# Softmax scores in three bf16 parts, four maxima units moved to the entry of the error attention, and routers on unnormalised rows, in a two-layer transformer kernel

## The chip, the core and the metric

The kernel runs on one core of one Trainium2 chip. A core has five engines that run their own instruction streams in order and meet only at semaphores: TensorE (PE, matrix products and transposes), VectorE (DVE), ScalarE (ACT), GpSimd (POOL) and SyncE (SP), which here issues nearly all DMAs. The metric is the device time of one execution in microseconds (us); the kernel before took a median of 610.33 us.

## The reference

Four sequences of 512 tokens with 128 features go through six steps, each on layer-normalised rows and added to the rows x:

```
x += 0.5 * ffn(norm(x))           # weights rounded to -1, 0, 1; exact gelu; 128 -> 512 -> 128
x += attention(norm(x))           # 16 heads of 8 features
x += 0.5 * ffn(norm(x))
x += 0.5 * experts(norm(x))       # 8 experts, relu, 128 -> 512 -> 128
x += linear_attention(norm(x))
x += 0.5 * experts(norm(x))
```

The attention is a sum of two. With q and k projected and v = the normalised rows, `y_ar = softmax(causal(q k^T / sqrt 8)) v`. The second works on the errors `e[t] = v[t+1] - y_ar[t]`: `y_ma = tril(qa ka^T) e`, where qa and ka are a leaky relu of q and a sigmoid of a third projection k2. Both go through one output projection.

In the experts step a router takes `softmax(row Wr)`, sends each of the 2048 tokens to its best expert, keeps the first 256 tokens of each expert in token order, and multiplies an expert's answer by the probability.

## The kernel before

**Stages.** Batch means one of the four sequences, tile 128 of its tokens. The entry (0 to 108 us of the profile) does the first feed-forward layer and the projections of all batches. The softmax attention follows batch by batch (to 162, 217, 272 and 312 us), then the second feed-forward layer with the first router (to 370), the experts (to 414), the linear attention with the second router at its end (to 566) and the second experts. The order of every engine is written out by hand in functions of the same name for each engine, such as `attention(b)` for PE (L1729), ACT (L902), DVE (L1238) and POOL (L691).

**Softmax scores.** A head has 8 features, so a full-precision product is made from halves: `split` (DVE, L1158) rounds q and k to float32r, `low_parts` (POOL, L638, through `low` at L601) takes the remainder. Each operand is written to DRAM three times by `stack` (SP, L363), as (high, low, high) for q and (high, high, low) for k, so that 24 contracted rows per head give high x high, low x high and high x low. A 25th row carries minus the maximum of the query's scores against a row of ones in DRAM, so that the exponent needs no other subtraction. Each head takes 32 of 128 partitions, and four heads make a set. One operand of a set stands as a block diagonal in `ring` (zeros cleared by POOL's `clear_ring`, L583), the other in `x_sets` or `m_sets`; the loads are `load_exp_set` (L368) and `load_max_set` (L376), five DMAs each. The zero and one rows in DRAM are stored at the start (L352 to L361).

**Maxima.** A query's maximum must be known before its scores are made. So PE makes all scores twice. In the first pass ten units of a set (pairs of a query tile and a key tile, 4 heads x 128 keys = 512 columns, `max_scores`, L1627) go through two PSUM banks, and DVE reduces each (`maxima`, L1169). The four units on the diagonal get a mask added by one more matmul, in bf16. For the first batch this is done in the entry, partly with four banks (`wide_scores`, `wide_maxima`); for batch b + 1 it is done beside the attention of batch b, placed by `MAX_BESIDE`. When all 40 units of a batch are reduced, `max_of_tiles` (DVE, L1186) makes the maximum over tiles, `max_turn` (PE, L1656) transposes it, `max_t` (ACT, L868) copies it out of PSUM, and `max_row` (SP, L414) writes the rows of maxima into `ring`.

**The loop.** For each set PE makes five units of two score matmuls (`scores`, L1662, two units ahead), ACT takes the exponent (L909), POOL clears the forbidden half of the diagonal (L669), and PE multiplies by the values (`answers`, L1674, groups of 8 small matmuls). Between these stand the maxima units of the next batch. `turn_answers` and `answers_divide` turn the answers of a set and divide them by their sums.

**Error attention.** After the last set, PE does `ma_scores(b, 0)`, turns the last answers, turns the maxima, turns y_ar (it waits for the copy of the maxima, since both use the bank `turn[1]`), and then goes through four tiles: state, `ma_scores` of the next tile, `ma_answers`. DVE masks the scores of each tile (L1267).

**Routers.** For each batch: moments (DVE, L1070), the reciprocal root on POOL (`rsqrt`, L587), `normalise` (L1075), transposes (PE), copy (ACT), `logits` (PE, L1571, fp32 matmuls of 8 columns), `choose` (DVE, L1105), `ranks` (PE, L1577), `place` (DVE, L1122), and `scatter` (POOL, L603, indirect DMAs that write the rows to their expert). In the first router PE does the transposes and logits of batch b - 1 inside `output` of batch b (`route`, L1782). In the second the last batch stands alone at the end of the linear attention (`turn_exit`, L2007). Where PE would be idle, `stay_awake(n)` (L1525) issues n bf16 matmuls of 512 columns whose result is not used.

## Time and profile before

| | |
|---|---|
| three runs | 607.28, 616.01, 610.33 us, median 610.33 |
| profiled execution | 613.04 us, its span 611.2 us |
| granted TensorE clock, mean over the span | 0.95 of full speed |
| busy: PE, DVE, ACT, POOL | 501.7, 340.9, 214.8, 243.7 us |
| chain that ended last | PE 55%, DVE 18%, POOL 7%, issue 6%, ACT 6%, DMA 5% |
| DMA | 79.86 MB, mean 131 GB/s |

Busy time and chain are of the one profiled execution; the span is from its first to its last instruction, and the execution's time has 1.8 us more. The chain is followed back from the last instruction, at each step to what released it. PEld is the loading of weights into PE, which can run beside a matmul. A matmul's end is modelled: those that follow each other overlap in the listing, so the distance between starts, not the duration, says what one costs.

### The profile page before, as it was taken

To read this page: it belongs to the slowest core of one execution; us is meant where nothing else is said; L and a number is where in the kernel's file an instruction comes from. 1 tells how busy PE (TensorE), PEld (TensorE's weight loads), DVE (VectorE), ACT (ScalarE), POOL (GpSimd) and SP (SyncE) were. 2 spreads that over 40 slices of the span, in tenths; PEclk is the share of its full clock that TensorE was granted. 3 is DMA by queue.
4 is the path that set the end of the run, shared out by engine and by line. 5 is a ranking of instruction groups with operands and counts; after the bars stand their busy time and mean duration, and the time that the engine had idled before them with its cause. 6 is when DMAs were issued, how large, how long until landed. Compare 5 with 4: busy or idle time off the path is not lost.

```text
span 611.2 us, 10402 instructions
## 1 busy us (share of the span) xinstructions
PE 501.7 (82%) x3827; PEld 321.1 (53%) x3827; DVE 340.9 (56%) x912; ACT 214.8 (35%) x298; POOL 243.7 (40%) x292
## 2 busy tenths in 40 slices
PE   0787776899999999989888978947887797898893
PEld 0564432444644654464467735943455575653692
DVE  4653586477487757752235651315697888842131
ACT  0446232554456455448644501202231311100120
POOL 5576365133342433336412465552221130332153
PEclk9996798899999999999999989998998999977997
DMA  8306989564156225405699322312857272111220
GB/s 258 154 22 198 314 249 294 153 187 123 34 133 186 63 62 157 121 17 154 156 155 261 112 96 86 105 38 76 237 160 192 68 223 80 54 52 36 87 64 10
DMA packets 73730, 79.86 MB, mean 131 GB/s; under 512 B 11010, under 2 KB 50563, under 8 KB 73424
## 3 DMA queue, kind: packets, MB, share of 16 engines
q1 hardware_dynamic: 70824, 73.15, 42.6%
q0 software_dynamic: 2560, 5.58, 2.6%
q8 instruction: 31, 0.51, 0.4%
q10 hardware_dynamic: 296, 0.47, 0.2%
q14 instruction: 19, 0.16, 0.1%
HBM read 44.07 MB, written 35.72 MB: 131 GB/s over the span
## 4 chain that ended last, share of the span: by engine, by line
PE 55%; DVE 18%; POOL 7%; issue 6%; ACT 6%; DMA 5%; SPq 2%; POOLq 0%; DVEq 0%; ACTq 0%
PE ps_pair L1514 18%; PE ps_accum L1514 16%; PE ps_max_pair L1514 15%; POOL sb_rstd L592 2%; DVE sb_work L1409 2%; DVE sb_stats L1070 2%; DVE sb_mpart L1173 2%; SPq L366 1%; PE ps_turn L1522 1%; POOL xe_scr L612 1%; PE ps_turn L1695 1%; PE ps_max_pair L1522 1%; DMA sb_cols<-in_bias_cols 1%; DMA sb_expert_rows<-xe_scr 1%; DVE sb_y_tmp L1079 1%
## 5 line engine op out<-in xcount | busy, mean ns | idle before, releaser
L1173 DVE TENSOR_REDUCE sb_mpart<-ps_max_pair 128x4 f32<-128x512 f32 x132 | 88.0, 688 | 41.2 <-PE ps_max_pair L1514 40.8
L909 ACT ACTIVATE sb_work<-ps_pair 128x1024 f32<-128x1024 f32 x80 | 81.1, 1025 | 61.5 <-PE ps_pair L1514 60.7
L1514 PE MATMUL ps_max_pair<-sb_ring,sb_m_sets 128*128 128x512 f32 x146 | 64.7, 471 | 8.9 <-DVE sb_mpart L1173 5.4
L669 POOL TENSOR_SCALAR_AFFINE_SELECT sb_work<-sb_work 128x512 f32<-128x512 f32 (+1 forms) x48 | 37.8, 790 | 65.7 <-ACT sb_work L909 65.7
L1514 PE MATMUL ps_pair<-sb_ring,sb_xsets 128*128 128x512 f32 x160 | 57.4, 445 | 3.5 <-ACT sb_work L909 1.4
L1514 PE MATMUL ps_pair<-sb_ident_bf,sb_ones_bf 128*128 128x512 bf16 x185 | 49.1, 421 | 12.3 <-DMA sb_x<-y_scr 8.0
L1514 PE MATMUL ps_accum<-sb_work,sb_v_aug 128*32 128x128 f32 (+3 forms) x768 | 57.9, 400 | 1.1 <-POOL sb_work L669 1.1
L1514 PEld LDWEIGHTS ps_max_pair<-sb_ring,sb_m_sets 128*128 128x128 f32 x146 | 27.0, 192 | 45.5 <-DVE sb_mpart L1173 28.1
L1409 DVE TENSOR_TENSOR sb_work<-ps_pair,sb_cst 128x1024 f32<-128x1024 f32 x32 | 37.5, 1213 | 2.5 <-PE ps_pair L1514 2.5
L1514 PEld LDWEIGHTS ps_pair<-sb_ident_bf,sb_ones_bf 128*128 128x128 bf16 x185 | 19.5, 108 | 35.5 <-issue 10.2
L612 POOL DMA_INDIRECT xe_scr<-sb_exit_rows,sb_slot_all x16 | 15.9, 996 | 54.5 <-DVE sb_slot_all L1154 50.8
L1514 PEld LDWEIGHTS ps_pair<-sb_ring,sb_xsets 128*128 128x128 f32 x160 | 28.1, 194 | 15.5 <-issue 6.6
L590 POOL TENSOR_SCALAR sb_ve<-sb_mv 128x4 f32<-128x4 f32 x24 | 5.5, 231 | 69.5 <-DVE sb_mv L1073 63.8
L1514 PE MATMUL ps_pair<-sb_y_tmp,sb_mw 128*128 128x256 f32 x128 | 30.7, 383 | 2.0 <-ACT sb_y_tmp L971 2.0
L1514 PEld LDWEIGHTS ps_accum<-sb_work,sb_v_aug 128*32 128x32 f32 x768 | 17.8, 113 | 23.9 <-issue 18.5
L1514 PE MATMUL ps_pair<-sb_xs,sb_w1r 128*128 128x512 f32 x64 | 22.2, 474 | 9.6 <-DVE sb_xs L1089 6.0
L1353 DVE TENSOR_SCALAR sb_work<-ps_pair 128x512 f32<-128x512 f32 x16 | 10.9, 681 | 27.6 <-PE ps_pair L1514 27.6
L1514 PEld LDWEIGHTS ps_pair<-sb_y_tmp,sb_mw 128*128 128x128 f32 x128 | 23.1, 190 | 5.5 <-ACT sb_y_tmp L971 3.0
L592 POOL TENSOR_TENSOR sb_rstd<-sb_ve,sb_cst 128x4 f32<-128x4 f32 x24 | 25.0, 1041 | 2.0
L1514 PE MATMUL ps_pair<-sb_ring,sb_ka_stk 128*128 128x512 f32 x64 | 22.1, 461 | 2.9 <-DVE sb_work L1409 2.4
L688 POOL TENSOR_SCALAR_AFFINE_SELECT sb_work<-sb_work 128x1024 f32<-128x1024 f32 x16 | 17.5, 1092 | 17.6 <-ACT sb_work L900 17.6
L1514 PE MATMUL ps_max_pair<-sb_add_q_bf,sb_ident_bf 128*128 128x512 bf16 x59 | 23.5, 398 | 0.0
(251 smaller groups left out, 981.2 us busy)
## 6 DMA issues: line engine op xcount, KB each, us to landing
sb_ka_stk<-mk_scr SPq DMA_DIRECT2D x16, 512.0 KB
sb_expert_rows<-xe_scr SPq DMA_DIRECT2D x16, 258.0 KB, 2.8
sb_m_sets<-q_scr SPq DMA_DIRECT2D x16, 256.0 KB
xe_scr<-sb_cst SPq DMA_DIRECT2D x4, 1024.0 KB, 13.0
sb_mw<-in_mw SPq DMA_DIRECT2D x16, 256.0 KB, 5.7
sb_xsets<-k_scr SPq DMA_DIRECT2D x15, 256.0 KB
q_scr<-sb_qs SPq DMA_DIRECT2D x12, 256.0 KB, 3.8
k_scr<-sb_ks SPq DMA_DIRECT2D x12, 256.0 KB, 4.0
```

The source lines that it names most:

```text
L366: sp.dma_start(scr[:, c], hi_lo[:, part, :].bitcast(F32)).then_inc(kept, 16)
L592: pool.tensor_tensor(rstd[i][:], ve[i][:], const("minus_half"), ALU.pow).then_inc(s["rstd"], 1)
L612: pool.indirect_dma_start(xe_scr[m], bass.IndirectOffsetOnAxis(ap=slot_all[:, i:i + 1], axis=0), rows_out[m][b][:, t, :], None).then_inc(s ...
L669: pool.affine_select(weights, weights, [[0, weights.shape[1]], [0, HL], [1, P]], ALU.is_ge, 0.0, base=0, channel_multiplier=-1).then_inc(s ...
L688: pool.affine_select(part, part, [[0, 2 * HL], [1, P]], ALU.is_ge, 0.0, base=-1, channel_multiplier=-1).then_inc(s["ma_zeroed"], 1)
L909: act.activation(unit_slots(i), pair[u % 2][:], ACT.Exp, scale=SCALE).then_inc(s["exp_done"], 1)
L1070: dve.bn_stats(stats[i][:, t, :], src[:, t, :]).then_inc(s["stats"], 1)
L1173: dve.tensor_reduce(mpart[:, m // NPAIR, m % NPAIR, :], max_banks[m % 2][:].rearrange("p (h k) -> p h k", h=HL), AX.X, ALU.max).then_inc(s ...
L1353: dve.tensor_scalar(work[:, n % 2, 1, :], pair[n % 2][:, 1, :], 0.0, None, ALU.max).then_inc(s["h_relu_v"], 1)
L1409: dve.tensor_tensor(work[:, n % 4].rearrange("p a (h q) -> p (a h) q", h=HL), pair[n % 2][:].rearrange("p a (h q) -> p (a h) q", h=HL), bc ...
L1514: return pe.matmul(dst, lhsT, rhs, start=start, stop=stop, skip_group_check=True)
L1522: last = pe.transpose(tile(dst, t), src[:, t, 0:D], ident)
```

## The change

1. **Scores.** q and k are kept as three bf16 parts (high, middle, least), whose sum is the float32 value. Six products (parts of 8 rows each, so 48 rows) replace three; a head takes 64 partitions, and two heads ("a half") stand in one matmul's block diagonal. The scratch in DRAM is bf16, each operand is stored by three DMAs of contiguous parts, and a set is loaded by four DMAs. The maxima become two bf16 rows (high and rest), which DVE makes by one copy and one subtraction more in `max_of_tiles`. POOL fills `x_sets` with ones, so the rows of ones and two of three rows of zeros in DRAM go. The middle part costs a subtraction and a cast per operand (`rest`), on DVE for batches 0 and 1, on POOL for 2 and 3.
2. **Units.** A maxima unit is one matmul of 2 heads x 256 keys (or two of 256 columns), a set has ten units with 18 matmuls, masks included, and 12 score matmuls. The columns per set stay at 12,288.
3. **Entry of the error attention.** Four units of the last set leave the loop: two stand before `ma_scores(b, 0)`, two after the turn of the last answers. Their reduces and `max_of_tiles` stand on DVE after the first mask and the first state, `max_turn` stands at tile 1 and has another bank, and y_ar is turned after `ma_scores` of tile 1.
4. **Routers.** Wr loses its column mean once (one matmul, one DVE operation), so that logits can be taken from rows that are not normalised: the choice of the expert needs no scale, and the logits are scaled before the exponent. Transposes and logits so follow the sum directly. In the first router the logits of batch b - 1 are made in the first step of the next output, the ranks in the third. In the second, the 27 idle matmuls before `turn_exit` become 4. The 32 idle matmuls ahead of each experts stage become 8 before the places, 24 after them and 14 after the scatter.

The core of the diff:

```diff
-MAX_PAIRS = [(qt, kt) for qt in range(NT) for kt in range(qt + 1)]
+MAX_UNITS = [(0, "3ab"), (0, "3cd"), (0, "2ab"), (0, "1ab"), (1, "3ab"), (1, "3cd"), (1, "2ab"), (1, "1ab"), (0, "2c0a"), (1, "2c0a")]
 MAX_BESIDE = [(1, 0, 0), (1, 1, 1), (1, 0, 0), (1, 0, 1), (1, 0, 2)]
+MAX_BESIDE_LAST = [(1, 0, 0), (1, 1, 1), (1, 0, 0), (1, 0, 0), (0, 0, 0)]
+MAX_LEFT = [NS * NPAIR - 4, NS * NPAIR - 2, NS * NPAIR]
...
-        q_scr = dram("q_scr", [B, H, 4, HD, T])
+        q_scr = dram("q_scr", [B, H, HD, PARTS, T], BF16)
...
+        def rest(eng, b, i):
+            full, parts, high, least = operands[i]
+            eng.wait_ge(s["split_hi"], 2 * b + i + 1)
+            if i == 0:
+                eng.wait_ge(s["ma_q"], b + 1)
+            eng.tensor_tensor(full[:], full[:], parts[:, high], ALU.subtract).then_inc(s["split_part"], 1)
+            eng.wait_ge(s["split_part"], 4 * b + 2 * i + 1)
+            eng.tensor_copy(parts[:, 1], full[:]).then_inc(s["split_part"], 1)
...
+            def stack_parts(parts, scr, kept, runs):
+                rows = scr.rearrange("h d c t -> (h d) c t")
+                for c, (first, last) in zip((0, 3, 5), runs):
+                    sp.dma_start(rows[:, c:c + last - first], parts[:, first:last]).then_inc(kept, 16)
...
             def load_exp_set(b, hs):
...
+                for j in range(HP):
+                    rows_of = slice(PR * j, PR * j + PARTS * HD)
+                    sp.dma_start(x_ring[rows_of, i, :, j], half_rows(q_scr, b, hs, j)).then_inc(done, 16)
+                    sp.dma_start(x_sets[rows_of, i], half_rows(k_scr, b, hs, j)).then_inc(done, 16)
...
             def low_parts(b):
+                if b >= 2:
+                    rest(pool, b, 0)
+                    rest(pool, b, 1)
+                for i, (full, parts, high, least) in enumerate(operands):
+                    pool.wait_ge(s["split_part"], 4 * b + 2 * i + 2)
+                    pool.tensor_tensor(parts[:, least], full[:], parts[:, 1], ALU.subtract).then_inc(s["split_lo"], 1)
...
-            clear_ring(0, 2)
+            clear(x_ring[:])
...
-            clear_ring(2, 3)
+            pool.memset(ring[:, 2].bitcast(F32), 0.0)
+            clear(m_ring[:, 0])
...
+            pool.wait_ge(s["ffn_h"], NF * B)
+            pool.memset(x_sets[:], 1.0).then_inc(s["x_ones"], 1)
             low_parts(B - 1)
...
             def max_of_tiles(b):
...
+                dve.tensor_copy(max_high[:], mneg[:, :, :, 0]).then_inc(s["max_parts"], 1)
+                dve.wait_ge(s["max_parts"], 2 * b + 1)
+                dve.tensor_tensor(mneg[:, :, :, 1], mneg[:, :, :, 0], max_high[:], ALU.subtract).then_inc(s["max_parts"], 1)
...
             def before_attention(b):   # DVE
                 if b:
                     split(b - 1, 0)
+                    query_features(b - 1)
                     split(b - 1, 1)
-                    query_features(b - 1)
+                    if b <= 2:
+                        rest(dve, b - 1, 0)
+                        rest(dve, b - 1, 1)
...
             def scaled_logits(r, norm):   # new, DVE
+                dve.wait_ge(s["rstd"], norm + 1)
+                dve.tensor_tensor(r8[1][:], r8[0][:], rstd[r % B % 2][:].unsqueeze(2).broadcast_to([P, NT, E]),
+                                  ALU.mult).then_inc(s["lg_scaled"], 1)
...
             def after_attention(b):   # DVE
                 ffn_x(B + b, x[b], old)
-                moments(norm_second(B + b), old, b % 2)
-                if b:
-                    choose(b - 1, accum[1])
-                normalise(norm_second(B + b), old, rows_out[0][b], b % 2)
+                n = norm_second(B + b)
+                moments(n, old, b % 2)
+                choose(b, accum[1])
+                normalise(n, old, rows_out[0][b], b % 2)
+                scaled_logits(b, n)
                 if b + 2 < B:
                     low(B + b + 2)
-                if b:
-                    place(b - 1, b - 1, accum[1], slot_all[:, NT * (b - 1):NT * b])
+                place(b, b, accum[1], slot_all[:, NT * b:NT * (b + 1)])
...
             def attention(b):   # PE, after the loop over the sets
+                if ahead:
+                    max_scores(b + 1, MAX_LEFT[0], MAX_LEFT[1])
                 ma_scores(b, 0)
                 turn_answers(b, NS - 1)
                 if ahead:
-                    max_turn(b + 1)
-                pe.wait_ge(s["y_norm"], NS * b + NS)
-                if ahead:
-                    pe.wait_ge(s["max_t_evac"], b + 2)
-                turn_tiles(turn[1], y_ar).then_inc(s["yar_mm"], 1)
+                    max_scores(b + 1, MAX_LEFT[1], MAX_LEFT[2])
...
                         ma_scores(b, t + 1)
+                    if t == 0:
+                        if ahead:
+                            pe.wait_ge(s["smax_red"], (NM + NT) * (b + 1) + MAX_LEFT[2] - 1)
+                        pe.wait_ge(s["y_norm"], NS * b + NS)
+                        turn_tiles(turn[1], y_ar).then_inc(s["yar_mm"], 1)
+                    elif t == 1 and ahead:
+                        max_turn(b + 1)
                     ma_answers(b, t)
...
             pe.wait_ge(s["experts_loaded"], 16 * 2 * E)
+            stay_awake(8, pair[1][:, 0])
             pe.wait_ge(s["rank_j"], B)
-            stay_awake(32, pair[1][:, 0])
+            stay_awake(24, pair[1][:, 0])
+            pe.wait_ge(s["scattered"], 16 * NT * B)
+            stay_awake(14, pair[1][:, 0])
             experts(0)
...
             project_out(B - 1)
-            stay_awake(27, pair[0][:, 0])
+            stay_awake(4, pair[0][:, 0])
             turn_exit(B - 1)
```

## Rows read from the trace of the kernel before

**Rows 1.** Page, part 1: busy us of each engine, share, instructions.

```profile
PE 501.7 (82%) x3827; PEld 321.1 (53%) x3827; DVE 340.9 (56%) x912; ACT 214.8 (35%) x298; POOL 243.7 (40%) x292
```

**Rows 2.** Windows: us, busy PE, PEld, DVE, ACT, POOL, clock, DMA share, GB/s.

```profile
75.00:95.00 20.00, 15.36 (x53) 6.95 (x51) 16.38 (x19) 7.84 (x13) 12.96 (x10) 0.99 0.82 248
163.00:203.00 40.00, 38.88 (x240) 18.41 (x238) 29.34 (x58) 22.14 (x23) 14.40 (x21) 1.00 0.49 139
...
540.00:567.00 27.00, 23.81 (x116) 11.97 (x115) 6.76 (x38) 1.99 (x4) 9.23 (x10) 0.81 0.15 50
```

**Rows 3.** Chain of waits, batch 1's sets: start us, us, what.

```profile
167.03 1.00 PE ps_accum L1514 x8
...
177.26 1.00 PE ps_accum L1514 x8
186.95 0.99 PE ps_accum L1514 x8
```

**Rows 4.** Timeline of PE inside one set: start us, us, instruction.

```profile
182.28 0.50 PE L1514 MATMUL ps_max_pair<-sb_ring,sb_m_sets 128*128 128x512 f32 x1
182.62 0.62 PE L1514 MATMUL ps_pair<-sb_ring,sb_xsets 128*128 128x512 f32 x2
183.08 0.39 PE L1514 MATMUL ps_max_pair<-sb_ring,sb_m_sets 128*128 128x512 f32 x1
```

**Rows 5.** Chain of waits through the second router.

```profile
546.34 5.83 PE ps_pair L1514 x27
552.17 0.45 PE ps_max_pair L1522 x4
...
553.28 1.07 PE ps_max_pair L1514 x8
...
555.52 0.52 PE ps_max_pair L1514 x14
...
565.91 2.73 DMA sb_expert_rows<-xe_scr
```

**Rows 6.** Page, part 5: count, then busy us, mean ns, idle before.

```profile
L1173 DVE TENSOR_REDUCE sb_mpart<-ps_max_pair 128x4 f32<-128x512 f32 x132 | 88.0, 688 | 41.2 <-PE ps_max_pair L1514 40.8
...
L1514 PEld LDWEIGHTS ps_max_pair<-sb_ring,sb_m_sets 128*128 128x128 f32 x146 | 27.0, 192 | 45.5 <-DVE sb_mpart L1173 28.1
...
L1514 PEld LDWEIGHTS ps_pair<-sb_ident_bf,sb_ones_bf 128*128 128x128 bf16 x185 | 19.5, 108 | 35.5 <-issue 10.2
```

**Rows 7.** Chain of waits through the first router's last batch.

```profile
350.56 0.70 DVE sb_wide_rows L1101
...
354.27 1.34 DVE sb_wide_rows L1079 x4
...
362.05 0.96 POOL xe_scr L612
```

**Rows 8.** Timeline of all engines where batch 0's error attention begins.

```profile
150.37 0.55 DVE L1191 TENSOR_REDUCE sb_mneg<-sb_mpart 128x16 f32<-128x16 f32 x4
...
152.34 0.63 PE L1522 MATMUL ps_max_pair<-sb_cst,sb_y_ar 128*128 128x128 f32 x4 [0.76 <-ACT sb_qs L876]
...
153.69 1.23 DVE L1267 TENSOR_TENSOR sb_work<-ps_pair,sb_cst 128x1024 f32<-128x1024 f32 x1 [0.17 <-PE ps_pair L1514]
...
155.29 1.17 PE L1514 MATMUL ps_pair<-sb_qa_pad,sb_ka_stk 128*128 128x512 f32 x4
```

**Rows 9.** Timeline of POOL in the entry: one of its fills.

```profile
24.14 1.81 POOL L585 MEMSET sb_ring<- 128x2048 f32 x1
```

**Rows 10.** Timeline of the entry: batch 2's remainder and its stores.

```profile
75.51 1.27 POOL L601 TENSOR_TENSOR sb_qs<-sb_qf,sb_qs 128x512 fp32r<-128x512 f32 x1 [5.94 <-DVE sb_qs L1162]
...
76.88 2.13 SPq L366 DMA_DIRECT2D q_scr<-sb_qs  x3
```

**Rows 11.** Chain of waits in the entry: a load of the last set.

```profile
91.75 3.90 DMA sb_m_sets<-q_scr
```

**Rows 12.** Timeline of PE: idle matmuls ahead of the second experts.

```profile
558.14 9.81 PE L1514 MATMUL ps_pair<-sb_ident_bf,sb_ones_bf 128*128 128x512 bf16 x32 [2.11 <-DVE sb_slot_all L1154]
```

More of the change, by code:

```diff
@@ L183, in build @@
         xs = [sb("xs_0", [P, 2, T], F32R)]
[L184 removed]
+        with nc.sbuf_tensor("sb_xsets", [P, 2, HP, T], BF16) as x_sets:
             pass
@@ L196, in build @@
         yT = w1
+        with nc.sbuf_tensor("sb_q_parts", [P, 3, T], BF16) as q_parts:
+            pass
+        with nc.sbuf_tensor("sb_max_rows", [P, T], BF16) as max_rows:
+            pass
         qs = sb("qs", [P, 2, T], F32R)
+        with nc.sbuf_tensor("sb_k_parts", [P, 3, T], BF16) as k_parts:
+            pass
         ks = sb("ks", [P, 2, T], F32R)
@@ L206, in build @@
             pass
+        with nc.sbuf_tensor("sb_x_ring", [P, 2, HP, HP, T], BF16) as x_ring, nc.sbuf_tensor("sb_m_ring", [P, 2, HP, HP, T], BF16) as m_ring:
+            pass
         ring = sb("ring", [P, NS, HL, T], F32R)
@@ L414, in max_row @@
             def max_row(b, hs):
-                sp.dma_start(ring[3 * HD:3 * HD + 1, hs % 2].bitcast(F32),
-                             mT[HL * hs:HL * hs + HL].bitcast(F32)).then_inc(s[f"xset{hs % 2}"], 16)
+                for j in range(HP):
+                    r = PR * j + PARTS * HD
+                    sp.dma_start(x_ring[r:r + 2, hs % 2, :, j], max_of_heads(hs, j)).then_inc(s[f"xset{hs % 2}"], 16)
             def keep_values(b):
@@ L743, in _ @@
             add_bias(norm_first(2 * B - 1), B - 1, 0, s["ffn_base"])
-            for b in range(2):
+            rsqrt(norm_second(B), 0)
+            for b in range(1, B):
+                scatter(0, b - 1, 0, 2)
                 rsqrt(norm_second(B + b), b % 2)
-            for b in range(2, B):
-                scatter(0, b - 2, 0, 2)
-                rsqrt(norm_second(B + b), b % 2)
-                scatter(0, b - 2, 2, NT)
-            for b in range(B - 2, B):
-                scatter(0, b)
+                scatter(0, b - 1, 2, NT)
+            scatter(0, B - 1)
             pool.wait_ge(s["rank_b"], 2 * B)
@@ L949, in _ @@
             act.wait_ge(s["max_t_evac"], 1)
-            act.dma_start(ring[3 * HD:3 * HD + 1, 0].bitcast(F32), mT[0:HL].bitcast(F32)).then_inc(s["xset0"], 16)
+            for j in range(HP):
+                r = PR * j + PARTS * HD
+                act.dma_start(x_ring[r:r + 2, 0, :, j], max_of_heads(0, j)).then_inc(s["xset0"], 16)
             act.wait_ge(s["mq_kept"], 48 * B)
@@ L1240, in attention @@
                 if b + 1 < B:
-                    at = [9] + [NPAIR * (hs + 1) + 3 for hs in range(NS - 1)] + [NM]
+                    at = [9] + [NPAIR * (hs + 1) + 3 for hs in range(NS - 1)] + [MAX_LEFT[1]]
                     maxima(b + 1, 0, 1)
@@ L1269, in attention @@
                                       bc(const("key_before"), 2 * HL), ALU.mult).then_inc(s["ma_masked"], 1)
+                    if t == 0 and b + 1 < B:
+                        maxima(b + 1, MAX_LEFT[1], MAX_LEFT[2])
                     if t < NT - 1:
@@ L1610, in before_attention @@
                 last = b == B - 1
+                if last:
+                    pe.wait_ge(s["wr_mid"], 1)
                 output(b, (lambda i: max_scores(0, i, i + 1)) if last else None)
@@ L1668, in scores @@
                     pe.wait_ge(s["exp_done"], NX * b + u - 1)
+                k_of, q_of = x_sets[:, hs % 2], x_ring[:, hs % 2]
                 for a in range(2):
-                    kt, qt = EXP_UNITS[i][a]
-                    last = mm(pair[u % 2][:, a, :], tile(x_sets[:, hs % 2], kt), ring[:, hs % 2, :, qt * P:(qt + 1) * P])
+                    if one_key_tile(i):
+                        kt, qt = EXP_UNITS[i][0]
+                        last = mm(pair[u % 2][:, a, :], tile(k_of[:, a], kt), q_of[:, a, :, qt * P:(qt + 2) * P])
+                    else:
+                        kt, qt = EXP_UNITS[i][a]
+                        for p in range(HP):
+                            last = mm(pair[u % 2][:, a, p * 2 * P:(p + 1) * 2 * P], tile(k_of[:, p], kt),
+                                      q_of[:, p, :, qt * P:(qt + 1) * P], start=p == 0)
                 last.then_inc(s["st_mm"], 1)
@@ L1743, in attention @@
                         scores(b, u + 2)
-                    m = NPAIR * hs + sum(map(sum, MAX_BESIDE[:i]))
-                    ends = [m + sum(MAX_BESIDE[i][:n]) for n in range(4)]
+                    beside = MAX_BESIDE if hs < NS - 1 else MAX_BESIDE_LAST
+                    m = NPAIR * hs + sum(map(sum, beside[:i]))
+                    ends = [m + sum(beside[i][:n]) for n in range(4)]
                     if ahead and (u or b == 0):
@@ L1791, in route @@
                         logits(b - 1, f - 1, accum[1], xnT[(b - 1) % 2])
+                    elif i == 2:
+                        ranks(b - 1, accum[1])
                 output(f, route if b else None)
```

292 lines of the change are left out of this document (160 added, 132 removed).

## The prediction, made before the changed kernel ran

> **What bounds the kernel now.** I read the summary of the page first: TensorE is busy for 82% of the span, VectorE for 56% [rows 1]. The table of stages says where that holds: in the attention (163 to 203 us) PE works 38.9 of 40 us, while in the entry (75 to 95) PE, VectorE and POOL work 15.4, 16.4 and 13.0 of 20, and in the router before the second experts (540 to 567) the clock is down to 0.81 of full speed [rows 2]; there engines take turns, and before the first experts too. The chain of waits then gives the pace. One set of four heads takes 9.7 us while the next batch's maxima are made beside it (177.26 to 186.95), and 10.2 us as the first of a batch (167.03 to 177.26) [rows 3]; the last batch's sets, which have no maxima beside them, are shorter. So the attention is priced on PE, and the other three places by their chains.
>
> **Scores in bf16 (A).** One set now issues 10 score matmuls and 10 maxima matmuls of 512 columns in float32r and 4 bf16 masks. The change issues 12 and 18 in bf16, some of 256 columns, but the columns are the same: 24 x 512. So only spacing can change. Two float32r matmuls that begin at 182.62 are followed by the next at 183.08, 0.23 us each; the first after a group of answers takes 0.34 (182.28 to 182.62) [rows 4]. 27 bf16 matmuls of 512 columns in a row take 5.83 us, 0.216 each, and 14 of 8 columns, each with its own weights, 0.52 us, 0.037 each; 8 of 8 columns in fp32 take 1.07, 0.13 each [rows 5]. So 20 x 0.02 = 0.4 us and five group heads x (0.11 - 0.04) = 0.35 us are to be had per set, less about 0.1 for six more matmuls: 0.65. VectorE gets none of this: ten reduces of 0.69 [rows 6] and a division keep it busy for 7.3 us of each 10 [rows 2], of what would be 9.04 us, and PE may be only two maxima ahead. I take 0.5. In the first set of batches 1 and 2 DVE also adds the last answers, takes moments and normalises (0.70 and 1.34 for the first and the last of these in [rows 7], the moments between them), which with 7.3 fills the 10.2, so no gain there. 10 x 0.5 + 4 x 0.4 in the last batch = **-6.6** (bounds: 0, if the reduces set the pace; -11, if all 16 sets get everything).
>
> The profile shows weight loads of 0.19 us in float32r and 0.11 in bf16, and that most of the former are hidden in the 0.23 [rows 4, 6]. The Trainium skill (TensorE: Matmul & The Clock Gate, sections Weight-path perf modes and Back-to-back issue gap) says that 128 weights not in fp32 load about twice as fast, and that load and matmul together set the spacing; the first agrees with the two rows, and by the second the whole difference would count, which is the first rival below.
>
> **Error attention (B).** Two of the four moved units leave the last set's loop (two matmuls with the waits around them, 0.5 each, so -1.0); they are issued where PE idles 0.76 us for the maxima's copy. But DVE now does, between its first mask and its second (153.69), two reduces (1.4), the reduction over tiles (0.55) and, new, a copy and a subtraction of 256 words (0.3 with their waits, an estimate) [rows 6, 8]. The second mask so ends some 1.5 us later than at 154.9, near 156.4, and PE, which needs it for the scores that begin at 155.29, waits 0.9 us; transposing the answers (0.45, as in [rows 5]) is no longer covered. The 32-row transpose has its own bank, and the rows of maxima land well before the next batch's scores. Net +0.3 for each of three batches, +0.45 in the last: **+1.3** (bounds: -2, if the stall is covered; +5, if none of the moved units is).
>
> **Entry (C).** In the first 43 us POOL's fills of 2048 float32 words take 1.81 us and stand right ahead of two rsqrt [rows 9]. The change adds a fill of 2048 bf16 words to each, and makes the fill of 4096 words before them (3.6 us by this row) one of bf16. If a fill goes by elements this is +3.6, if by bytes +1.8 - 1.8 = 0; no row has a bf16 fill of any size, so I take +2.0, between the two. The middle part costs two subtractions and two casts per batch. On DVE a pass over 512 float32 words takes 0.70 [rows 7], a cast perhaps 0.4, so 2.2 us for each of batches 0 and 1; DVE is busy for 16.4 of 20 us later in this stage [rows 2], and I let a quarter through, +1.0. For batches 2 and 3 they are on POOL, whose subtraction took 1.27 [rows 10]. For batch 2, SP waits for it to store q at 76.88; q's three stores would start 4.7 us later (two subtractions of 1.27, two casts of an estimated 1.1), and behind them stand the loads of set 2, the feature stores and the load of set 3 (the chain's DMA of 3.90 us at 91.75), which releases PE at 95.7 [rows 10, 11]. The three stores each keep their bytes, a set needs four loads (384 KB) instead of five (448 KB), so some 1.7 us of the 4.7 is won back: +3.0. The DMA engines are 82% busy here [rows 2], and 2 MB of zeros are not stored any more: -1.0 for shorter landings. The fill of ones, batch 3's four operations and the later fills are covered by that load and what follows it, since the scores start near 108 us. Together **+5.0** (bounds 0 and +18: both batches' POOL work in full, 4.7 and 4.7 with 1 for the fill of ones, the fills by elements, 3.6, and DVE's 4.4). The router's centred weights (one small matmul, one DVE operation, hidden by the fills' wait) and a second DMA for each row of maxima (on a queue with slack of a whole set) cost nothing.
>
> **Routers (D).** In the first, the last batch's rows wait after their sum (350.56, 0.70) for moments, POOL's rsqrt and a normalise of 1.34 at 354.27, and only then come transposes, copy, logits, choice, ranks and places; scatters start at 362.05 [rows 7]. Unnormalised, the transposes follow the sum at 351.26 directly, and the steps take what the second router shows: transposes 0.45, copy 0.6 (552.62 to 553.28), logits 1.07, choice 1.1 (554.35 to 555.52), ranks 0.52 and places 2.1 (556.04 to 558.14) [rows 5, 12]. 351.26 + 0.45 + 0.6 + 1.07 + 1.1 + 1.34 (normalise, ranks beside it) + 0.2 (scaling) + 2.1 and 0.3 of gaps is 358.4, and rsqrt runs beside it. But the earlier batches' choices now wait for logits inside the next output, ahead of DVE's places and sum; by the same rows the last sum is 1.0 us later. Gain 2.7. In the second, PE runs 27 idle matmuls (5.83) between projection (546.34) and transposes (552.17), and places are done at 558.14 [rows 5, 12]. After 546.34: 0.7 (sum) + 0.45 + 0.6 + 1.07 + 1.1 + 1.1 (normalise) + 0.2 + 2.1 + 0.3 of gaps = places at 553.9 instead of 558.1, so 4.2. Together **-6.9** (bounds: -9; +1, see the second rival). The 14 idle matmuls behind the scatter take 3.0 us at 0.216, about as long as the rows take to come (2.73 for the last DMA [rows 5], and its issue).
>
> **Sum.** -6.6 + 1.3 + 5.0 - 6.9 = -7.2 us. The profiled execution took 613.0 us (span 611.2 and 1.8 around it), which gives 605.8; it is 2.7 above the median of the three runs, 610.3, which gives **603 us**.
>
> **Rivals.** *Weight loads count in full.* 0.19 - 0.11 on 20 loads is 1.6 to 1.7 us per set, 12 sets and half as much in four: A = -24, time **586**. For it: five heads of groups per set expose 0.11. Against: within a run 0.23 holds load and matmul. The Trainium skill's rule on spacing, named above, is this one. 0.15.
>
> *VectorE paces, and the routers' gain is lost.* A falls to -1.5, since 7.3 us of reduces and division with two banks leave PE waiting; and the choice of batch b, which waits for logits inside the next output, makes DVE the bound of the feed-forward stage; or PE is granted the lower clock (the 32 idle matmuls at 558.14 took 9.81, 0.31 each, clock 0.81 in this stage [rows 2, 12]) and 14 more take 6 us, 3 too many: D = -2. Then **613**. So the scores would be cheaper on an engine that isn't the limit. 0.22.
>
> *POOL becomes the entry's bound.* Place: between the last split and SP's stores, 75 to 108 us. If nothing of it is covered C is 18 and the time **616**, slower. It decides from C = 12.2, that is, from an attention that starts later than about 120 us. Against: POOL is busy 13 of 20 us there [rows 2], and SP's own queue, not POOL, fills the chain from 77 to 91 us. 0.10.
>
> **Numbers.** Forecast 0.53, on its own 596 to 609. A measurement of this kernel can tell about 2%, 12 us, from no change. Faster by more (under 598): the first rival's 0.15 and a quarter of the forecast's, 0.28. Slower by more (over 622.5) takes the third rival together with A near 0: 0.04. Within: 0.68. The range 590 to 614 leaves out most of the first rival and the third.
>
> **What would show it.** A: sets of about 9.2 us, 0.22 between matmuls, PE's weight loads near 0.1; sets still at 9.7 with PE waiting for the reduce say the second rival, under 8.5 the first. B: PE waiting for DVE's second mask near 8 us after the last answers. C: first scores at about 113 us; at 108 or less my price of POOL was wrong, over 120 the third rival is right. D: scatters of the last batch 2 to 4 us sooner after the sum, places 8 us after the last projection. The forecast fails if attention and entry both come out on one side of their terms.

## The result, and the profile after

| | before | after |
|---|---|---|
| median of 20 runs, us | 610.38 (607.28 to 617.09) | 614.66 (610.81 to 618.41) |
| ratio, 95% interval | | 1.0053 (1.0031 to 1.0076) |
| profiled execution, us | 613.04, span 611.2 | 611.52, span 609.8 |

The change makes the kernel slower, by 0.3 to 0.8% (of the two medians, 4.3 us); 603 was forecast, in a range to 614. The profiled execution of after is among the fastest of its twenty and that of before among the slower ones, so the two traces are compared stretch by stretch and not by their sums.

Page after, part 1 (the columns of [rows 1]). PE is 17.6 us less busy; the time does not follow, so PE now waits somewhere.

```profile
PE 484.1 (79%) x3917; PEld 300.6 (49%) x3917; DVE 348.2 (57%) x937; ACT 214.9 (35%) x301; POOL 254.8 (42%) x303
```

Windows of after, for the stretches of [rows 2]: entry, attention, second router.

```profile
75.00:95.00 20.00, 17.13 (x58) 7.18 (x56) 12.64 (x15) 6.90 (x11) 13.31 (x13) 0.82 0.61 200
168.00:208.00 40.00, 36.41 (x264) 14.83 (x264) 29.11 (x58) 22.31 (x24) 15.02 (x22) 1.00 0.51 129
541.00:566.00 25.00, 21.70 (x133) 11.29 (x126) 7.88 (x47) 1.98 (x4) 9.23 (x10) 0.89 0.20 66
```

In the attention PE was busy for 38.9 of 40 us, now for 36.4. The chain of waits through one set of batch 1 shows what took PE's place; in [rows 3] the set from 177.26 to 186.95 held PE alone.

```profile
183.81 0.26 DVE sb_rcp L1298
...
184.09 0.30 DVE sb_y_ar L1300
...
184.47 0.46 POOL sb_e_pad L727
184.93 0.41 POOL sb_v_next L728
185.34 1.07 POOL sb_work L715
...
186.55 0.43 PE ps_accum L1593 x8
...
194.88 1.06 POOL sb_work L715
```

PE's answers wait for POOL's clear of the forbidden half (L715); that stands on POOL behind two subtractions (`errors`, L727 and L728), which wait for DVE's division of the set before. From clear to clear it is 9.54 us, the period of the later sets of a batch: only 0.15 less than the 9.69 of [rows 3]. The timeline of after shows the same clear with its shape and PE's wait (start, us, instruction, in brackets the idle time ahead and its releaser).

```profile
185.08 0.60 PE L1593 MATMUL ps_pair<-sb_x_ring,sb_xsets 128*128 128x512 bf16 x2
185.30 1.10 POOL L715 TENSOR_SCALAR_AFFINE_SELECT sb_work<-sb_work 128x1024 f32<-128x1024 f32 x1
185.52 0.38 PE L1593 MATMUL ps_max_pair<-sb_m_ring,sb_m_sets 128*128 128x512 bf16 x1
186.55 0.43 PE L1593 MATMUL ps_accum<-sb_work,sb_v_aug 128*32 128x128 f32 x8 [0.54 <-POOL sb_work L715]
```

It clears 1024 columns, two blocks of the diagonal at once. The starts at 185.08 and 185.52 answer to [rows 4]: two bf16 matmuls in 0.44 us, 0.22 each, as forecast. The weight loads fell to 0.1 us (page after, part 5, against 192 and 108 ns in [rows 6]).

```profile
L1593 PEld LDWEIGHTS ps_max_pair<-sb_m_ring,sb_m_sets 128*128 128x128 bf16 x176 | 15.7, 99 | 50.4 <-DVE sb_mpart L1236 21.5
```

In the entry, the first exponent starts at 116.05 us instead of 108.67. The chain of waits of after shows where: a fill of 2048 bf16 words, the stores of batch 2, the last load (they answer to [rows 9 to 11]: 1.81 us, 76.88, 91.75), and behind the load the last step of the maxima (L1259) and two DMAs that ACT issues for the rows of maxima (L999).

```profile
25.67 1.80 POOL sb_m_ring L627
...
80.48 1.16 POOL sb_qf L362
...
81.70 0.68 POOL sb_q_parts L364
82.38 1.13 POOL sb_kf L362
...
83.56 0.61 POOL sb_k_parts L364
84.17 1.13 POOL sb_q_parts L687
...
85.38 0.33 SPq L407
...
97.46 3.69 DMA sb_m_sets<-q_scr
...
109.19 0.44 DVE sb_mneg L1259 x4
...
111.84 1.23 ACTq L999
...
116.05 1.95 ACT sb_work L957 x2
```

The last step of the maxima and the first exponent in the chain of waits of before:

```profile
103.59 0.55 DVE sb_mneg L1191 x4
...
108.67 1.03 ACT sb_work L909
```

Both routers became shorter. The chain through the last batch of the first (to [rows 7]): from the start of the sum to the first scatter 8.6 us.

```profile
357.54 0.70 DVE sb_wide_rows L1148
...
366.18 0.96 POOL xe_scr L654
```

In before it was 12.8. The row at 362.05 in [rows 7] is not the last batch's first scatter: the trace has five scatters from there on and a batch has four, so it is batch 2's last, and the last batch's first stands behind it on POOL (chain of waits of before):

```profile
363.31 0.96 POOL xe_scr L612
```

And through the second (to [rows 5]): from the end of the last projection (548.46) to the first matmul of the experts 19.8 us, where before had 23.4 (546.34 to 569.72).

```profile
548.46 0.86 PE ps_pair L1593 x4
...
556.94 1.09 POOL xe_scr L654
...
568.26 1.99 PE ps_pair L1593 x8
```

The same matmul in the chain of before:

```profile
569.72 1.99 PE ps_pair L1514 x8
```

### The profile page after: what moved, and what is told of

It reads as the page before. It is cut to its first block, busy times and chain, and to the rows that moved or that the text cites. A ratio compares the mean times of both kernels' runs of the same rounds, so it can differ in the third digit from the quotient of the medians.

```text
span 609.8 us, 10598 instructions
## 1 busy us (share of the span) xinstructions
PE 484.1 (79%) x3917; PEld 300.6 (49%) x3917; DVE 348.2 (57%) x937; ACT 214.9 (35%) x301; POOL 254.8 (42%) x303
## 4 chain that ended last, share of the span: by engine, by line
PE 42%; DVE 24%; POOL 12%; issue 7%; ACT 6%; DMA 5%; SPq 2%; POOLq 0%; ACTq 0%; DVEq 0%
PE ps_pair L1593 14%; PE ps_accum L1593 13%; PE ps_max_pair L1593 11%; DVE sb_work L1486 3%; POOL sb_work L715 2%; POOL sb_rstd L634 2%; DVE sb_stats L1117 2%; ACT sb_work L957 2%; DVE sb_mpart L1236 1%; POOL xe_scr L654 1%; DMA sb_expert_rows<-xe_scr 1%; DVE sb_work L1340 1%; PE ps_max_pair L1601 1%; DVE sb_mpart L1233 1%; PE ps_turn L1601 1%
## 5 line engine op out<-in xcount | busy, mean ns | idle before, releaser
L957 ACT ACTIVATE sb_work<-ps_pair 128x1024 f32<-128x1024 f32 x80 | 79.7, 1025 | 59.4 <-PE ps_pair L1593 59.2
L1236 DVE TENSOR_REDUCE sb_mpart<-ps_max_pair 128x2 f32<-128x512 f32 x106 | 70.7, 687 | 32.3 <-PE ps_max_pair L1593 30.9
L715 POOL TENSOR_SCALAR_AFFINE_SELECT sb_work<-sb_work 128x512 f32<-128x512 f32 (+1 forms) x48 | 37.8, 788 | 64.2 <-ACT sb_work L957 63.9
L1593 PE MATMUL ps_accum<-sb_work,sb_v_aug 128*32 128x128 f32 (+3 forms) x768 | 56.6, 394 | 10.1 <-POOL sb_work L715 8.9
L1593 PE MATMUL ps_max_pair<-sb_m_ring,sb_m_sets 128*128 128x512 bf16 (+1 forms) x176 | 55.4, 354 | 10.5 <-DVE sb_mpart L1236 4.3
L1593 PE MATMUL ps_pair<-sb_ident_bf,sb_ones_bf 128*128 128x512 bf16 x177 | 45.9, 411 | 12.9 <-DMA sb_x<-y_scr 8.0
L1593 PE MATMUL ps_pair<-sb_x_ring,sb_xsets 128*128 128x512 bf16 (+1 forms) x192 | 47.1, 345 | 4.0 <-ACT sb_work L957 1.8
L1593 PEld LDWEIGHTS ps_max_pair<-sb_m_ring,sb_m_sets 128*128 128x128 bf16 x176 | 15.7, 99 | 50.4 <-DVE sb_mpart L1236 21.5
L1593 PEld LDWEIGHTS ps_pair<-sb_ident_bf,sb_ones_bf 128*128 128x128 bf16 x177 | 18.0, 105 | 34.7 <-DMA sb_x<-y_scr 8.1
L1593 PE MATMUL ps_max_pair<-sb_add_q_bf,sb_ident_bf 128*128 128x256 bf16 (+1 forms) x88 | 28.1, 319 | 0.0
L1593 PEld LDWEIGHTS ps_pair<-sb_x_ring,sb_xsets 128*128 128x128 bf16 x192 | 16.1, 97 | 23.5 <-issue 8.9
```

The costliest lines, as they stand in the source:

```text
L715: pool.affine_select(weights, weights, [[0, weights.shape[1]], [0, HL], [1, P]], ALU.is_ge, 0.0, base=0, channel_multiplier=-1).then_inc(s ...
L957: act.activation(unit_slots(i), unit_scores(u), ACT.Exp, scale=SCALE).then_inc(s["exp_done"], 1)
L1236: dve.tensor_reduce(mpart[:, slot, h:h + HP, p], bank.rearrange("p (j k) -> p j k", j=HP), AX.X, ALU.max).then_inc(s["smax_red"], 1)
L1593: return pe.matmul(dst, lhsT, rhs, start=start, stop=stop, skip_group_check=True)
```

## The experiments

**1. POOL's subtractions behind the clear** (errors_late).

```diff
                     clear_late(b, hs, 1)
-                    errors(b, hs - 1)
                     clear_late(b, hs, 2)
+                    errors(b, hs - 1)
```

> The changed kernel, but POOL clears the last diagonal unit of a set before it subtracts the answers from the values (errors), not behind it. Theory 1 (the unit order of the change put POOL on the chain: division on DVE, two subtractions of 0.46 and 0.41 on POOL, a clear of two blocks of 1.06, then the answers): the two subtractions leave the chain, sets of 9.54 us become about 8.9, sets of the last batch 7.0 become about 6.1; time about 606.5 against 614.7 of the changed kernel. Theory 2 (DVE's ten reduces and its division pace the sets): sets stay at 9.5 and the last batch's at 7.0; time about 614.

Measured: 604.3 us, ratio to before 0.9909 (0.9867 to 0.9952), that is 10.4 below the changed kernel (8.8 by the ratios). In the timeline of ACT of this kernel the first exponents of batch 1's last two sets stand 8.93 us apart:

```profile
183.19 1.02 ACT L957 ACTIVATE sb_work<-ps_pair 128x1024 f32<-128x1024 f32 x1 [0.30 <-PE ps_pair L1593]
...
192.12 1.02 ACT L957 ACTIVATE sb_work<-ps_pair 128x1024 f32<-128x1024 f32 x1 [0.30 <-PE ps_pair L1593]
```

Its window over that set shows PE busy all the time:

```profile
183.20:192.10 8.90, 8.89 (x67) 3.63 (x66) 7.13 (x12) 5.58 (x6) 3.25 (x5) 1.00 0.61 183
```

Theory 1 holds in the full sets; neither DVE (7.1 of 8.9) nor POOL sets the pace any more. In the last batch one part failed: its third set stays at 7.3 us, since the rows of maxima land late, as its chain of waits says:

```profile
282.97 5.36 DMA sb_x_ring<-sb_max_rows
...
288.38 0.62 PE ps_pair L1593 x2
```

Where the 10.4 us lie is seen in the last group of the error attention's answers, in the chains of waits of after and of this kernel:

```profile
317.48 1.08 PE ps_accum L1593 x32
308.15 1.08 PE ps_accum L1593 x32
```

From the first exponent (116.05 and 115.12) it is 201.4 and 193.0 us, so 8.4 us are in the attention: in each of the first three batches 0.6 in the third set and 1.5 from the last set to the next batch, and the rest in the last batch. The other 2 us are no larger than the interval.

**2. The grouping of score units as before** (units_old).

```diff
-EXP_UNITS = [((0, 0), (0, 1)), ((0, 2), (0, 3)), ((2, 2), (2, 3)), ((1, 1), (3, 3)), ((1, 2), (1, 3))]
+EXP_UNITS = [((0, 0), (0, 1)), ((0, 2), (0, 3)), ((2, 2), (3, 3)), ((1, 1), (2, 3)), ((1, 2), (1, 3))]
```

> The changed kernel with the grouping of score units of the kernel before: (2,2) with (3,3) and (1,1) with (2,3). It issues 14 score matmuls per set instead of 12, and the last clear is of one block (0.63 us) and is needed only by the last group of answers. Theory 1 (the new grouping put POOL's clear on the chain): the last batch's sets fall from 7.0 to about 6.2, full sets from 9.54 to about 9.3; time about 611. Theory 2 (the bf16 scores or DVE pace the sets, whatever the grouping): no set is shorter, full sets even 0.1 longer for the two matmuls more; time 615 to 616.

Measured: 603.7 us, ratio 0.9895 (0.9857 to 0.9932). Sets again of 8.93 us, the last batch's third of 6.24. The subtractions are still ahead of the last clear, but that is now of one block and no answers wait for it soon (timeline of POOL):

```profile
190.76 0.46 POOL L727 TENSOR_TENSOR sb_e_pad<-sb_v_next,sb_y_ar 128x128 f32<-128x128 f32 x1 [1.54 <-DVE sb_y_ar L1300]
191.18 0.46 POOL L728 TENSOR_TENSOR sb_v_next<-sb_v_next,sb_y_ar 128x128 f32<-128x128 f32 x1
191.59 0.64 POOL L715 TENSOR_SCALAR_AFFINE_SELECT sb_work<-sb_work 128x512 f32<-128x512 f32 x1
```

So it takes both, the new grouping and the order on POOL, to make the chain: either edit alone cuts it. The gain is larger than expected (611), because the whole chain leaves and not only 0.4 us of it.

**3. The entry of the error attention as before, in the changed kernel (entry_back) and in that of experiment 1 (el_entry_back).** The first edit puts the maxima units back into the loop and the turns back to their places; the second adds the edit of experiment 1.

```diff
-                    beside = MAX_BESIDE if hs < NS - 1 else MAX_BESIDE_LAST
-                    m = NPAIR * hs + sum(map(sum, beside[:i]))
+                    m = NPAIR * hs + sum(map(sum, MAX_BESIDE[:i]))
...
-                if ahead:
-                    max_scores(b + 1, MAX_LEFT[0], MAX_LEFT[1])
                 ma_scores(b, 0)
                 turn_answers(b, NS - 1)
                 if ahead:
-                    max_scores(b + 1, MAX_LEFT[1], MAX_LEFT[2])
+                    max_turn(b + 1)
+                pe.wait_ge(s["y_norm"], NS * b + NS)
...
+                turn_tiles(turn[1], y_ar).then_inc(s["yar_mm"], 1)
```

> The changed kernel with the entry of the error attention as before: all maxima units in the loop, their reduction before the first mask, the turn of y_ar behind that of the maxima. Theory 1 (the moved units delay DVE's second mask, and the turn of y_ar is not covered in the last batch): 0.3 us less for each of three batches and 1.1 in the last, about 2 in all; time about 612.7. Theory 2 (the moved units free the loop and pay for themselves): the last sets get their 1.0 us back each, time about 616.

> The kernel of errors_late with the entry of the error attention as before the change (all maxima units in the loop). Theory 1 (moving the four units is worth something by itself, also when POOL's chain is cured: PE does them where it waited): from the first exponent of a batch's last set to the next batch 26.4 instead of 25.4 us, time about 607 against 604.3. Theory 2 (they paid only because POOL's chain left PE idle in the loop): 25.4 to 25.7, time 604 to 605.

Measured: 616.2 us (1.0087, 1.0051 to 1.0123), 1.6 above the changed kernel, and 605.5 us (0.9907, 0.9853 to 0.9961), 1.2 above experiment 1. The first is the time that theory 2 of the first text gives, but not its 1.0 us per set: from the last set to the next batch it is 27.2 us there and 27.0 in after. Medians that near to each other don't decide alone, but the traces do: with POOL's chain cured, a batch needs 25.9 us from the first exponent of its last set to that of the next batch with the old entry (195.22 to 221.14) and 25.4 with the new one (192.12 to 217.54). The two first exponents of the old entry, in the timeline of ACT:

```profile
195.22 1.02 ACT L955 ACTIVATE sb_work<-ps_pair 128x1024 f32<-128x1024 f32 x1 [0.30 <-PE ps_pair L1587]
...
221.14 1.02 ACT L955 ACTIVATE sb_work<-ps_pair 128x1024 f32<-128x1024 f32 x1 [2.96 <-PE ps_pair L1587]
```

So the moved units are worth 0.5 us per batch by themselves, half of what theory 1 of the second text asked for. PE does wait for DVE's second mask, as forecast, but only 0.3 us (timeline of PE in experiment 1):

```profile
209.31 1.19 PE L1593 MATMUL ps_pair<-sb_qa_pad,sb_ka_stk 128*128 128x512 f32 x4 [0.30 <-DVE sb_work L1340]
```

**4. The routers alone** (routers_only), on the kernel before: part 4 of the change and nothing else.

> The kernel before with the routers of the change alone (unnormalised rows, centred weights, fewer and split idle matmuls); scores, entry and error attention as before. Theory 1 (the three shortenings seen in the trace, 2.8 us in the first router, 1.7 in the linear attention and 3.6 in the second, belong to the routers): about 8 us less than before, 602.4. Theory 2 (what the trace shows in the linear attention is the clock of one execution, and the second router gives back part in a slower landing): 4 to 5 us less, about 606.

Measured: 601.8 us, ratio 0.9844 (0.9804 to 0.9883), 9.4 below before. The second router takes 19.4 us from the last projection to the experts (540.98 to 560.36), 4.0 less than before, about what theory 1 expects; but the 1.7 us of the linear attention do not belong to the routers, as theory 2 said: that stretch, from the first experts to the start of the last projection, took 171.4 us in the trace of before, 169.7 in after and 172.6 here.

```profile
540.98 0.86 PE ps_pair L1519 x4
...
560.36 2.00 PE ps_pair L1519 x8
```

Not all of the 9.4 us belongs to the routers: in the trace 2.8 of it lie ahead of them, where the last group of the error attention's answers begins at 308.11 us instead of 310.94, and the edit changes nothing there but the centring of Wr. From these answers to the first experts it is 3.8 us less than before.

**5. The routers with the idle matmuls as before** (routers_awake).

```diff
-            stay_awake(4, pair[0][:, 0])
+            stay_awake(27, pair[0][:, 0])
             turn_exit(B - 1)
...
-            stay_awake(24, pair[1][:, 0])
-            for left in sent[1]:
-                pe.wait_ge(left, 16 * NT * B // 2)
-            stay_awake(14, pair[1][:, 0])
+            stay_awake(32, pair[1][:, 0])
```

> The kernel of routers_only with the idle matmuls as before the change: 27 ahead of the second router's transposes, 32 behind the places in both. Theory 1 (in the second router the gain is the 23 idle matmuls that are gone; unnormalised rows alone move rsqrt and normalising from behind them onto DVE's chain after the choice): from the last projection to the first matmul of the experts 24 to 24.6 us instead of 19.4, time about 606.5 against 601.8. Theory 2 (the idle matmuls pay for themselves by a higher clock in the experts): 602 to 603.

Measured: 607.3 us (0.9942, 0.9906 to 0.9977), about 5 above experiment 4. Its second router takes 24.0 us, and the chain of waits has the 27 matmuls again:

```profile
534.36 5.83 PE ps_pair L1519 x27
540.18 0.45 PE ps_max_pair L1527 x4
```

So in the second router the gain is the idle matmuls. How many of them could have gone with normalised rows no run shows, but it can be worked out from the trace of before: there the normalised rows were ready at 551.22 us (timeline of DVE) and the transposes began at 552.17 [rows 5].

```profile
550.10 1.12 DVE L1079 TENSOR_SCALAR sb_exit_rows<-sb_exit_rows,sb_mv,sb_rstd 128x128 f32<-128x128 f32 x4 [1.59 <-POOL sb_rstd L592]
```

Fewer idle matmuls alone would thus have won about 1.0 of the 4.0 us, and the other 3 take unnormalised rows; this is an estimate and not run.

**6. The fills of the entry** (el_fills), on the kernel of experiment 1: the bf16 rings are cleared as float32 words, and the fills of the float32 ring come later.

```diff
-            clear(x_ring[:])
+            clear(x_ring[:].bitcast(F32))
...
-            pool.memset(ring[:, 2].bitcast(F32), 0.0)
-            clear(m_ring[:, 0])
+            clear(m_ring[:, 0].bitcast(F32))
...
             values(0)
+            pool.memset(ring[:, 2:4].bitcast(F32), 0.0)
```

> The kernel of errors_late with shorter fills in the entry: the bf16 rings are cleared as float32 words (half as many), and the two fills of the float32 ring that nobody needs before the linear attention stand behind the values of batch 0. Theory 1 (a fill goes by elements, and these stand ahead of the reciprocal roots that the entry's chain waits for): about 5 us less on POOL before 45 us, of which the chain gives back 3; first exponent at about 112 instead of 115.1, time about 601.5 against 604.3. Theory 2 (what the entry waits for later, the stores of batch 2 and the loads behind them, takes it back): first exponent at 115, time 604.

Measured: 600.5 us (0.9829, 0.9776 to 0.9882), 3.8 below experiment 1; the two intervals still touch. The first exponent is at 110.18, 4.9 sooner, with PE's granted clock at 0.97 from 75 to 95 us against 0.87 there. The same bytes as half as many words take half the time (timeline of POOL, after first, then this kernel; the second fill took 1.80 us in after):

```profile
9.51 3.50 POOL L627 MEMSET sb_x_ring<- 128x4096 bf16 x1
...
9.57 1.79 POOL L627 MEMSET sb_x_ring<- 128x2048 f32 x1
...
21.69 0.95 POOL L627 MEMSET sb_m_ring<- 128x1024 f32 x1
```

**7. The middle parts of batch 2 on DVE**, behind the operand of the next feed-forward step, on the kernel of experiment 1 (el_mid) and with experiment 6 (el_all).

```diff
-                    if b <= 2:
-                        rest(dve, b - 1, 0)
-                        rest(dve, b - 1, 1)
                 if b + 2 < B:
                     low(b + 2)
+                if b:
+                    rest(dve, b - 1, 0)
+                    rest(dve, b - 1, 1)
```

> The kernel of errors_late with the middle parts of batch 2 on DVE instead of POOL, and on DVE behind the operand of the next feed-forward step (low) instead of ahead of it. Theory 1 (POOL's four operations hold back the stores of batch 2, which start at 85.4 instead of 76.9, and DVE's hold back PE): stores about 3 us sooner, first exponent at about 112.5, time about 602. Theory 2 (DVE, which reduces the first batch's maxima there, becomes late by the same 2 us): first exponent at 114.5 to 115.5, time 604.

> errors_late with the edits of el_fills and el_mid together. Theory 1 (they shorten different stretches of the entry's chain): first exponent at about 109.5, time about 598.7. Theory 2 (one covers the other, the last set's load ends the entry either way): first exponent at 112, time about 601.

Measured: alone 603.7 us (0.9877, 0.9831 to 0.9922), which can't be told from experiment 1; with the fills 597.8 (0.9780, 0.9733 to 0.9826), 2.7 below experiment 6, first exponent at 107.9. The trace of the first can't settle it: its first exponent is at 117.2, but PE had a granted clock of 0.72 from 75 to 95 us there, against 0.87 in experiment 1 and 1.00 in the kernel with both edits. Together with the fills the median is lower, but the intervals overlap and the traces don't bear it out: there the second set of batch 0 begins at 116.23 us against 116.75 in experiment 6, since the first set's two leading score matmuls ran at a granted clock of 0.50, the lower level (1.02 us instead of 0.60; PE had stood idle from 98 to 100 us before the clock fell), and the two profiled executions took 598.8 and 598.4. What the middle parts are worth on DVE is not shown.

**8. The best version** (el_best): the second kernel of experiment 7, the keys of the last batch loaded one set later, and the second row of the very first maxima issued by SP. A variant (el_best_units) has the old grouping on top.

```diff
-                    elif hs == 1:
+                    if hs == (1 if b + 1 < B else 2):
                         load_keys(b, 0, 2)
                         load_keys(b, 2, NS)
```

> The kernel of el_all with two edits to SP's queue: the keys of the last batch's error attention are loaded one set later, and the second row DMA of the very first maxima is issued by SP, not behind the first on ACT. Theory 1 (the last batch's set 3 waits 1.5 us for its rows of maxima because 1 MB of keys lands beside them; two issues in a row on ACT cost 0.6 us): third set of the last batch 5.9 instead of 7.0 us, first exponent 0.6 sooner; time about 596.1 against 597.75. Theory 2 (the keys then come late for the error attention, or the rows are slow for another reason): third set at 7.0, or a wait of 1 to 2 us ahead of the error attention; time 598 to 599.

> The kernel of el_best with the grouping of score units of the kernel before (14 score matmuls per set, one block in the last clear). Theory 1 (once POOL's subtractions stand behind the clear, the grouping is no longer on the chain, and two matmuls more cost PE 0.1 to 0.2 us): sets 8.9 to 9.0, from the last set to the next batch 25.4 to 25.6; time 0 to 3 us above el_best. Theory 2 (the shorter clear still counts at the end of each batch): from the last set to the next batch 25.0, time 1 to 2 us below.

Measured: 595.6 us, ratio to before 0.9767 (0.9732 to 0.9802), and 596.4 (0.9763, 0.9732 to 0.9794): the two can't be told apart, so the grouping is about free once POOL's order is mended. From the last set to the next batch the variant takes 25.85 us against 25.43, a little above what theory 1 allowed. Of the two edits to SP's queue little is seen. The first exponent starts at 108.9, not sooner than the 107.9 of experiment 7. The third set of the last batch takes 6.65 us instead of 7.04, still waiting for its rows (chain of waits), so the keys were not all that held them.

```profile
276.31 4.67 DMA sb_x_ring<-sb_max_rows
...
281.03 0.62 PE ps_pair L1592 x2
```

What else holds them is left open.

## Why the prediction was wrong

**Scores in bf16 (A), the step that failed.** The prediction said of the new matmuls "the columns are the same", "so only spacing can change", and gave 0 as the worst. It counted the matmuls of a unit and did not ask who waits for it: the wait of the answers for POOL's clear stood at nothing. In the changed kernel A came out at +0.2: from the first to the last exponent 187.2 us with the new scores (entry_back, which has the old entry of the error attention) and 187.0 with the old ones (experiment 4). The new list puts (1,1) and (3,3) into one unit, the fourth; so the answers of key tile 3, which were ready after the third unit, and those of tile 1 now share one clear of 1.06 us, and on POOL that stood behind the subtractions, which wait for a division that DVE does after a reduce. Experiments 1 and 2 break this chain at two places, and both are 10 to 11 us faster, 8.4 and 7.5 of it seen between first exponent and last answers. None of the rivals held it: the second had VectorE pace the sets, but the reduce is only the first link, and with POOL's order changed the same reduces allow 8.93 us.

With the chain cut, the price of A was right in sum: 180.8 us from the first to the last exponent (el_entry_back), so -6.2 where -6.6 was forecast. That is partly luck. In the trace of experiment 1 against that of experiment 4, which has the old scores: sets of 8.93 instead of 9.69 us, that is 0.76, of which 0.65 had been counted and 0.5 taken; the sets beside which VectorE also normalises stay at 10.2 (10.3 with the old scores), as forecast; and the last batch, forecast at -1.6, won 0.2 (24.8 against 24.9 us), because its third set waits for the rows of maxima (6.9 against 6.2 us). The first rival, weight loads in full, asked for 8.0 and is out: the loads fell by 0.09 us and the spacing by 0.01. The Trainium skill's rule for it (TensorE: Matmul & The Clock Gate, Back-to-back issue gap) does not hold in these rows, and its sustained 0.131 us for 512 columns isn't seen in any of them.

**Error attention (B), sign wrong, size small.** +1.3 was forecast; experiment 3 gives -0.5 for each of three batches and +0.4 in the tail of the last (13.42 against 12.99 us from the last exponent to the last answers): -1.1, within the bounds. The wait for the second mask was priced at 0.9 us and is 0.3, since the scores that need it begin later as well (6.6 us behind the first error scores, without the wait, against 6.0 before).

**Entry (C), mis-sized, and one term left out.** +5.0 was forecast; the first exponent moves by 7.4 from before to after and by 7.8 (107.3 to 115.1) from experiment 4 to experiment 1, with a clock in this stage that differs from trace to trace. The chains of before and after show the terms. When POOL begins with batch 2's parts (75.51 in before [rows 10], 80.48 in after) 5.0 us are lost already, 3.0 forecast. The fills are a part of it: they go by elements (1.80 us for 2048 bf16 words, 1.81 for as many of float32), the upper end of what was bounded, 3.6, and I took 2.0. The Trainium skill says it of VectorE (VectorE: DVE Perf Modes, Zero memsets can be issued as uint32), one cycle per element whatever the type; the rows of experiment 6 show for POOL, too, that the time goes by elements. POOL's four operations on batch 2 hold its stores back by another 3.5, 4.7 forecast, as a cast, for which there was no row, takes 0.6 to 0.7 us there and not 1.1. The last load lands 5.5 us late, so 3.0 were won back (2.7 forecast). Behind it 1.9 us were lost where nothing was priced: from the last step of the maxima to the first exponent it takes 6.9 us instead of 5.1, with a copy and a subtraction more, a slower transposition (1.05 against 0.62, at a granted clock of 0.50 against 1.00) and two row DMAs that ACT issues in 1.23 us. The second row DMA was said to cost nothing; but when SP issued it (experiment 8) the first exponent did not come sooner.

**Routers (D), right.** -6.9 was forecast. Experiment 4 measures -9.4 (-12 to -7), and in its trace -6.5 without the 2.8 that lie ahead of the routers: 3.8 in the first, 4.0 in the second (4.2 forecast), 1.3 given back in the linear attention between them. The first was forecast at 2.7; there the prediction took 362.05 for the last batch's first scatter, which was 1.3 us later. The choices did wait inside the next output as said, and the last sum came 0.4 us later, not 1.0.

**Sum.** Scores, error attention and entry together cost 614.7 - 601.8 = 12.8 us where -0.3 was forecast. POOL's chain is 10.4 of it by the medians and 8.4 by the traces (experiment 1). The other 2.5, experiment 1 against 4, is no larger than the intervals of the two; in their traces the last group of the error attention's answers begins at 308.15 and 308.11 us. So without the chain the three terms nearly add up to the forecast, but by luck: the entry's +7.8 stands for +5.0, and -7.8 for the -5.3 of scores and error attention. Up to these answers the changed kernel is 9.4 us behind experiment 4 (317.48 against 308.11); the other 3.4 of the 12.8 are in no trace. The range ended 0.7 us short: it held the second rival's 613, with A at -1.5 and the entry as priced, and not A near 0 together with an entry 2.8 us dearer.

## What to carry to other kernels

When work is regrouped, follow every consumer of a group and not only the cost of its members: a group is ready when its last member is, and an engine that is 40% busy paces the loop if one of its instructions stands in order behind a slow producer. Where a faster format doesn't pay, look at the chain of waits for the engine that took the place of the old bound; here one line moved on POOL gave 8 to 10 us. Clear buffers of narrow words on POOL through a view of wider ones.

## What the runs showed of the hardware

A fill on POOL goes by elements, not by bytes: 4096 bf16 words took 3.50 us, and the same bytes as 2048 float32 words 1.79. A cast of 512 float32 words to bf16 took 0.61 to 0.68 us on POOL and 0.42 on DVE (trace of after). PE's 512-column matmuls follow each other at 0.22 us in bf16 and 0.23 in float32r, although the weight load fell from 192 to 99 ns. The granted clock in the entry differs from execution to execution (0.72 to 1.00 of full speed between 75 and 95 us in the kernels above, means of its two levels 0.50 and 1.00), and with one trace of each kernel no edit can be held to explain it.
